# One launch of five blocks on one core: TensorE's order in the first four units and at the join of tower and attention, constants around the relay's end, VectorE's order before the scores

## What is computed

```python
h = L0_tok(tokens)                     # embedding, a decaying memory, 4 x (layer norm, 128->512 gelu, 512->128), head 128->64
h = h + L0_attn(layernorm(h))          # fast weights: q, k, v, rk, rv, beta, rbeta from one projection
h = h + L0_ffn(layernorm(h))           # 8 experts, 2 chosen for a sequence
h = h + L1_attn(layernorm(h))          # 8 heads; softmax of scores mixed with a positional softmax
h = h + L1_ffn(layernorm(h))           # 8 experts, 2 chosen for a token

# L0_attn, over the 16 rows in order (per head)
W = W + (bt * (vt - W @ kt)) * kt ;  z = W @ qt                 # fast memory
q_rec = softmax(hid) ; R = R + (bt * (vt - R @ kt)) * kt        # second memory
hid = z + R @ q_rec ;  out = hid @ out_W
```

## Time and profile before

| | us |
|---|---|
| median of 3 runs | 646.36 (645.65 to 647.98) |
| the profiled execution, device time | 644.59 |
| its span in the trace | 642.8 |
| PE busy in it | 566.9 (88%) |
| DVE, ACT, POOL busy | 426.9, 351.3, 350.2 |

### The profile page before, as it was taken

The page is one execution under the profiler, slowest core; times in us unless marked ns, Lnnn a source line. Parts: engine busy times, 40 slices in busy tenths (PEclk is TensorE's granted clock), DMA queues, the critical chain, the costliest instruction groups (busy, mean ns, idle before and its releaser), DMA issues.

```text
span 642.8 us, 12533 instructions
## 1 busy us (share of the span) xinstructions
PE 566.9 (88%) x4564; PEld 428.9 (67%) x4564; DVE 426.9 (66%) x1092; ACT 351.3 (55%) x914; POOL 350.2 (54%) x469
## 2 busy tenths in 40 slices
PE   7979999999899785777788878899998799999996
PEld 3547777777335674566777768786567577786686
DVE  4934564324766786899898888997226966666533
ACT  1064444442786763226787968730764557757430
POOL 1597663311810776879998999982666310001435
PEclk9979999999999999699999989999899899999999
DMA  7000000000000434200000000000000000000000
GB/s 277 8 1 1 2 0 1 1 1 1 1 1 2 75 77 65 77 0 2 2 1 2 0 2 1 2 1 1 1 1 2 2 1 2 1 2 2 6 12 17
DMA packets 10861, 10.45 MB, mean 16 GB/s; under 512 B 6000, under 2 KB 9840, under 8 KB 10544
## 3 DMA queue, kind: packets, MB, share of 16 engines
q1 hardware_dynamic: 8080, 7.54, 4.2%
q0 software_dynamic: 2144, 1.75, 1.5%
q10 hardware_dynamic: 576, 0.35, 0.2%
HBM read 5.77 MB, written 0.52 MB: 10 GB/s over the span
## 4 chain that ended last, share of the span: by engine, by line
PE 59%; DVE 16%; ACT 9%; POOL 6%; issue 4%; DMA 3%; SPq 1%; DVEq 0%; POOLq 0%; ACTq 0%
PE bank L1256 9%; PE bank L1244 8%; PE bank L1333 7%; PE bank L1548 5%; PE bank L1589 4%; DVE bank L2035 3%; DVE features L2029 2%; PE bank L1293 2%; PE bank L1496 2%; PE bank L1647 2%; PE bank L1303 2%; DVE features L2005 2%; PE bank L1324 1%; PE bank L1635 1%; SPq L450 1%
## 5 line engine op out<-in xcount | busy, mean ns | idle before, releaser
L1333 PE MATMUL bank<-ident,features 128*128 128x128 f32 x604 | 80.0, 284 | 10.3 <-DVE features L2005 5.6
L1333 PEld LDWEIGHTS bank<-ident,features 128*128 128x128 f32 x604 | 70.4, 147 | 17.5 <-DVE features L2005 11.5
L855 ACT ACTIVATE G<-bank,cols 128x512 f32<-128x512 f32 x64 | 43.6, 686 | 53.2 <-PE bank L1244 53.2
L1244 PE MATMUL bank<-xs,weights 128*128 128x512 f32 x128 | 60.5, 617 | 2.4 <-ACT xs L846 2.3
L590 POOL TENSOR_TENSOR features<-UV,coefs 128x1024 f32<-128x1024 f32 (+3 forms) x36 | 59.7, 1673 | 2.2 <-DVE UV L1992 2.2
L1256 PE MATMUL bank<-weights,G 128*128 128x128 f32 x512 | 59.8, 275 | 0.0
L1256 PEld LDWEIGHTS bank<-weights,G 128*128 128x128 f32 x512 | 58.4, 192 | 0.0
L2005 DVE TENSOR_TENSOR features<-UV,bank 128x1024 f32<-128x1024 f32 (+3 forms) x68 | 55.6, 861 | 1.6 <-PE bank L1333 0.8
L390 POOL TENSOR_SCALAR rstd<-mv 128x4 f32<-128x4 f32 x8 | 1.6, 194 | 96.2 <-DVE mv L402 96.2
L940 ACT ACTIVATE xs<-UV,coefs 128x32 f32<-128x32 f32 x232 | 50.3, 308 | 0.0
L940 ACT ACTIVATE sx<-UV,coefs 128x32 f32<-128x32 f32 x200 | 43.4, 307 | 0.0
(11 more groups left out here) (355 smaller groups left out, 1399.8 us busy)
## 6 DMA issues: line engine op xcount, KB each, us to landing
weights<-in_w SPq DMA_DIRECT2D x2, 1024.0 KB, 9.9
features<-in_tok SPq DMA_DIRECT2D x1, 768.0 KB, 5.9
weights<-in_ew SPq DMA_DIRECT2D x4, 128.0 KB, 3.3
weights<-in_ew SPq DMA_DIRECT2D x2, 256.0 KB, 3.0
coefs<-G POOLq DMA_DIRECT2D x16, 25.5 KB, 4.9
rows<-in_rows SPq DMA_DIRECT2D x1, 384.0 KB, 6.4
out_h<-H SPq DMA_DIRECT2D x3, 128.0 KB, 2.0
coefs<-G SPq DMA_DIRECT2D x14, 25.5 KB, 4.7
```

Of the source, the lines that this page charges most:

```text
L855: act.activation(G[:, 4 * (w % 2) + f, :], up_bank(f)[:], ACT.Gelu, bias=col("b1", 4 * i + f)).then_inc(s["tok_gelu"], 1)
L1244: mm(up_bank(f)[:], w1[:, i, P * f:P * f + P], xT[:, w % 2, :], start=True, stop=True).then_inc(s["tok_up"], 1)
L1333: last = mm(out[:, P * k:P * k + P], x[:, P * k:P * k + P], ident[:], is_transpose=True, start=first and k == 0, stop=last_ and k == n - 1 ...
```

## The change

Nothing is computed otherwise; orders on three engines change, and constants.

1. Units 0 to 3: ScalarE takes the gelus of unit 0 ahead of `unit_first(1)`, and in units 1 and 2 `unit_first` and `evict_T` stand between gelus. TensorE runs down(0) in two halves on either side of turn(1).
2. The join: `normalised(0)` goes ahead of down(15); the heads of chunks 2 and 3, with VectorE's parts and `a_norm(1)` to `a_norm(3)`, go between the features of chunks 0 and 1. ScalarE runs one exponential of a single column right after the last gelu.
3. Constants: at the relay 10 and 3 become 8, 4 (after a new wait for the softmax's factors) and 5; steps 0, 1, 2 get 4, 2, 2 behind the `rec` reads; row 12's third piece of `held` gets 6 ahead of it; in the scores 3 ahead of the loop and 2 after `turn_scores(0)` and `turn_scores(1)`.
4. Scores: VectorE takes `d_apply(1)` after `normalise(0)`, and `add_experts(3)` and what follows it one row later. TensorE's wait for that addition moves from ahead of the loop to `values_back(0)`.

```diff
@@ ACT
             evict_T(0)
-            for w in range(NU):
-                if w + 1 < NC:
-                    unit_first(w + 1)
+            gelus(0)
+            unit_first(1)
+            evict_T(1)
+            for w in range(1, NC - 1):
+                gelus(w, 0, 2)
+                unit_first(w + 1)
+                gelus(w, 2, 3)
+                evict_T(w + 1)
+                gelus(w, 3, 4)
+            for w in range(NC - 1, NU):
...
-            for c in range(1, NC):
-                head(c)
+            act.activation(decay[:, 3:4], ones[:, 0:1], ACT.Exp).then_inc(s["decay_exp"], 1)
+            head(1)
             normalised(0)
...
@@ PE
                 if w == 0:
                     embed(3)
+                    down(0, 0, 2)
...
-                if w:
+                if w == 0:
+                    down(0, 2, CH)
+                elif w > 1:
                     down(w - 1)
...
             head(1)
+            normalised(0)
             down(NU - 1)
-            for c in range(2, NC):
-                head_turn(c)
-                head(c)
...
+                    if t == 12 and r0 == 2 * CH:
+                        pe.wait_ge(s["o_add"], t - 1)
+                        warm(6)
                     pe.wait_ge(s["held_p"], i + 1)
...
-            for k in range(10):
-                mm(held_sum[:, HB:2 * HB], ident[:], RK[:, 0, :], start=True, stop=True)
+            constants(held_sum[:, HB:2 * HB], 8)
+            pe.wait_ge(s["p_done"], 1)
+            constants(held_sum[:, HB:2 * HB], 4)
             pe.wait_ge(s["p_done"], 2)
...
+            constants(held_sum[:, HB:2 * HB], 5)
...
                 read_out("rec", t, reads_of("rec", t))
+                if t < 3:
+                    pe.wait_ge(s["o_add"], t)
+                    warm((4, 2, 2)[t])
...
             fold_sums(3)
-            pe.wait_ge(s["y_read"], NC)
+            constants(bank[6][:, HB:2 * HB], 3)
...
                 turn_scores(t)
+                if t < 2:
+                    constants(bank[6][:, HB:2 * HB], 2)
@@ DVE
             for c in range(NC):
                 feature(c, 0)
                 feature(c, 1)
                 read_keys(CH * c)
+                if c == 0:
+                    a_norm(1)
+                    head(2)
+                    a_stats(2)
+                elif c == 1:
+                    a_norm(3)
...
                 f1_apply(c)
-                if c:
-                    d_apply(c - 1)
+                if c == 1:
+                    d_apply(0)
...
                 normalise(t)
                 if t == 0:
+                    d_apply(1)
+                if t == 1:
                     add_experts(chunk[NC - 1])
                     f1_stats(NC - 1)
```

More of the change, by code:

```diff
@@ L847, in evict_T, with gelus @@
                                scale=col("ln_g", i)).then_inc(s["tok_hT"], 1)
-            def gelus(w):
+            def gelus(w, f0=0, f1=4):
                 i, c = unit(w)
-                for f in range(4):
+                for f in range(f0, f1):
                     act.wait_ge(s["tok_up"], 4 * w + f + 1)
@@ L981, in _ @@
                     turned_keys(c - 1, 0)
+                else:
+                    head(3)
                 feature(c, 2)
@@ L1245, in up, with down @@
                        start=True, stop=True).then_inc(s["tok_up"], 1)
-            def down(w):
+            def down(w, j0=0, j1=CH):
                 i, c = unit(w)
@@ L1253, in down @@
                     pe.wait_ge(s["tok_add"], w - 1)
-                for j in range(CH):
+                for j in range(j0, j1):
                     for f in range(4):
@@ L1257, in down @@
                                   w2[:, i, f, :], start=(f == 0), stop=(f == 3))
-                last.then_inc(s["tok_down"], 1)
+                if j1 == CH:
+                    last.then_inc(s["tok_down"], 1)
             def head_turn(c):
@@ L1264, in head_turn @@
                     pe.wait_ge(s["head_xT"], c)
+                if c == 2:
+                    pe.wait_ge(s["a_turned"], 2)
                 for j in range(CH):
@@ L1279, in normalised @@
                 pe.wait_ge(s["a_norm"], c + 1)
-                pe.wait_ge(s["head_xT"], NC)
+                pe.wait_ge(s["head_xT"], NC if c else 2)
                 if c:
@@ L1423, in _ @@
             head(1)
+            normalised(0)
             down(NU - 1)
-            for c in range(2, NC):
-                head_turn(c)
-                head(c)
             pe.wait_ge(s["load_attn"], 64)
             pe.wait_ge(s["pad"], 1)
-            normalised(0)
             pe.wait_ge(s["tok_gelu"], 4 * NU)
-            pe.wait_ge(s["tok_add"], NU)
             for c in range(NC):
@@ L1435, in _ @@
                 feature(c, 1)
+                if c == 0:
+                    head_turn(2)
+                    pe.wait_ge(s["tok_add"], NU - 1)
                 values_keys(CH * c)
@@ L1438, in _ @@
                     turn_keys(c - 1, 0)
+                else:
+                    head(2)
+                    head_turn(3)
                 feature(c, 2)
+                if c == 0:
+                    pe.wait_ge(s["tok_add"], NU)
                 values_keys(CH * c + 1)
@@ L1469, in _ @@
                 last.then_inc(s["p_T"], 1)
-            for k in range(3):
-                mm(held_sum[:, HB:2 * HB], ident[:], RK[:, 0, :], start=True, stop=True)
+            constants(held_sum[:, HB:2 * HB], 5)
             def queries(t):
@@ L1666, in values_back @@
                 pe.wait_ge(s["av_saved"], p + 1)
+                if p == 0:
+                    pe.wait_ge(s["y_read"], NC)
                 if p % 2 == 0 and p:
@@ L2152, in _ @@
             a_stats(0)
+            a_norm(0)
             add(NU - 2)
-            a_norm(0)
             head(1)
@@ L2157, in _ @@
             add(NU - 1)
[L2158 to L2164, removed]
             for c in range(NC):
@@ L2168, in _ @@
                 read_keys(CH * c)
+                if c == 0:
+                    a_norm(1)
+                    head(2)
+                    a_stats(2)
+                elif c == 1:
+                    a_norm(3)
                 feature(c, 2)
                 read_keys(CH * c + 1)
+                if c == 0:
+                    head(3)
+                    a_stats(3)
                 feature(c, 3)
@@ L2173, in _ @@
                 read_keys(CH * c + 3)
+                if c == 0:
+                    a_norm(2)
             dve.wait_ge(s["rk_T"], 2 * NC)
@@ L2389, in _ @@
                 if t == 0:
+                    d_apply(1)
+                if t == 1:
                     add_experts(chunk[NC - 1])
                     f1_stats(NC - 1)
-                if t == 1:
+                if t == 2:
                     f1_apply(NC - 1)
                     d_stats(NC - 2)
-                if t == 2:
+                if t == 3:
                     d_apply(NC - 2)
-                if t == 3:
+                if t == 4:
                     d_stats(NC - 1)
-                if t == 4:
+                if t == 5:
                     d_apply(NC - 1)
```

## The result

In the first comparison the changed kernel took 639.58 us (median of 4 runs, 637.23 to 640.11) beside 647.17 for the kernel before (645.65 to 650.42): a ratio of 0.9857, interval 0.9818 to 0.9896. The profiled execution took 639.34 with a span of 637.6, so the two profiles differ by only 5.25. The forecast was a gain of 5.8.

A forecast was written before the change was run, and what follows sets the result against it. TensorE, busy 88%, was taken to set the pace mostly, with waits and half clock in early tower, join, recurrence and first scores; 1.6 - 3.5 - 0.3 - 0.85 - 2.75 = -5.8 from 646.36 gives 640.6, range 638.2 to 643.9.

The forecast's parts named there:

- The tower: Units 0 to 3: new order keeps 0.4 us of 4.4, half clock behind turn(4)'s wait costs 2.0; together +1.6.
- The rival that turn(4) does not wait: Tower: GpSimd's list runs earlier than thought, all 4.4 us stay, 634.6; chance 0.04.
- The join: Down(15) to chunk 1's features: they start 4.1 us sooner, less VectorE's norm delay; -3.5 taken.
- Relay and steps 0 to 2: Recurrence start: constants hold the clock, shortening the relay's constants and step 1; together -0.3 us.
- The first rival: Recurrence: constants do not hold the clock and cost double, +3.0 in place of -0.3, 643.9; chance 0.14.
- The rule of the Trainium skill: Recurrence: transpose mode does not engage full clock, so it falls between few constants; would give 643.9 rather than 640.6.
- Row 12: Recurrence: six constants fit the 3.15 us idle, transposes and turn behind run at full clock; -0.85 us.
- Scores: First scores: reordered norm, no TensorE wait or half clock, less two pairs of constants; -2.75 us.
- the base of 646.36: Whole kernel: median of the runs before, 1.77 above the profiled 644.59, from which the forecast subtracts 5.8.

The follow-up runs named there:

- e2: Changed kernel with GpSimd's fills of constants moved behind its root for unit 8: 635.39, ratio 0.9806 to the kernel before.
- e8: Changed kernel with VectorE's norms of chunks 2 and 3 one chunk later: 640.02, ratio 0.9876 to the kernel before.
- e4: Changed kernel with the join of before put back: ratio 0.9942 to the kernel before.
- e3: Changed kernel without the two pairs of constants behind the turned scores of rows 0 and 1: 639.25, ratio 0.9855 to the kernel before.
- c2: Changed kernel run again with nothing edited: 640.76, ratio 0.9889 to the kernel before.
- e6: Changed kernel without the six constants ahead of row 12's third piece: ratio 0.9891 to the kernel before.
- e1: Changed kernel with the old order of units 0 to 3 on ScalarE and TensorE: ratio 0.9872 to the kernel before.
- e7: Changed kernel with the first scores of before (VectorE's order, TensorE's wait, no constants there): ratio 0.9912 to the kernel before.
- c3: Kernel before, unchanged, profiled again: join and step 11 as in its first profile, relay 3.3 us longer; no run time given.
- c4: Kernel before, unchanged, profiled again: join 51.83 us, half clock twice as long in step 11; no run time given.
- e5: Changed kernel with the constants of before around the relay (ten and three) and none in steps 0 to 2: ratio 0.9863 to the kernel before.

## Why the prediction was right in its places and wrong in its sum

**The tower** went as written: turn(4) at 58.17 (forecast 58.25), behind an idle 3.82, with the half clock on turn(4) and down(2); up(4), at 64.75, ran at full clock again. The first profile has +2.2 to the end of the tower, the means of the table +1.6 (six towers in the old order 147.8, eight in the new 149.4): the term, +1.6. In the first profile the half clock lasted for 6.8 us there, in the seven others for 3.4. The rival that turn(4) does not wait is out, by e2, which had to remove the wait to see it go.

**The join** gave 2.7 where 3.5 was forecast from the first profile. The forecast was 4.1 less 0.6 for VectorE's norm, and 0.8 is missing. The start of chunk 1's features before, and the first two features of the changed kernel:

```profile
172.96 1.99 PE L1293 MATMUL bank<-coefs,sx 128*128 128x512 f32 x4
```
```profile
160.24 1.88 PE L1307 MATMUL bank<-coefs,sx 128*128 128x512 f32 x4
```

Counted from the last gelu, chunk 1's features start at 24.46 before and at 20.84 now: 3.6 earlier, not 4.1. TensorE, busy throughout, needed 11.3 from the end of down(15) at 160.24 to 171.57 for the list that was added up to 10.7; from one start to the next a head took 0.94, not 0.84. So 0.5 of the 0.8 is TensorE's own list, too small. The other 0.3 lies behind that point: there the new order loses 0.9, of which e8 gives back 0.68, the norm beside GpSimd, within the 0.3 to 1.3 that it was given and close to the 0.6 that was taken. But in three of five profiles of before, and in e4, the half clock falls into the old join, with its gaps between head and head; in none of the eleven profiles with the new heads between the features did it fall there. Against the mean of the old joins (51.65) the new one is worth 3.7. The term came out right by errors that cancel, which is luck.

**Relay and steps 0 to 2**: -0.3 was forecast, +0.1 measured (steps 0 to 4, means 38.10 and 38.16). The first rival's condition was met in part, in six of the eleven profiles with these constants: the clock was down on the two of step 1 in five of them (1.70 to 1.92 for 1.03, as in the row at 268.44) and on the four of step 0 in e3:

```profile
263.86 3.02 PE L1522 MATMUL bank<-RK,ident 128*128 128x256 f32 x8
```

Its price was too high: the stage took 37.87 to 38.18 in the five and 38.78 in e3, where c2 and e6, with the clock up all through it, took 37.79 and 37.80. That is 0.1 to 0.4 and 1.0, not 1.2 and 1.8. The 39.69 of e2 has another place: there the clock fell at 275.3, in step 3, on constants that the kernel before has as well. The rule of the Trainium skill that stood beside that rival (TensorE: Matmul & The Clock Gate, Part 4, PE-mode transpose) is not settled here: the rise at 275.0 goes against it; the falls in these steps, among transposes, could go with it.

**Row 12** was forecast at -0.85; the first two profiles give -0.99, and the means of steps 4 to 15 -1.5 (145.37 in six kernels without the constants, 143.89 in eleven with them). The price of that gap was taken from one half-clock stretch; in four of the six it lasted twice as long. Against that, the clock fell on step 12's own constants in two of the eleven (e1, e7).

**Scores**: -2.75 forecast, -2.80 measured, in the first pair and in the means.

**The step that failed** is that one profile of before stood for all of its runs, in the terms and in the sum: "The median of the runs is 1.77 above it; I make the forecast against the median". That takes the profiled execution as typical and its distance to the median as the same for both kernels. Of 64 runs of before 4 are shorter than its 644.59; the median is 3.5 above it. That of the changed kernel is 0.6 above its own. So the 5.25 that the profiles show, near the 5.8, became 8.1. That 5.25 is near 5.8 is itself in part luck: 0.93 of it lies in the experts, which the change does not touch, and the other stages make -4.3 (+2.2, -2.7, -0.1 for the relay with steps 0 to 4, -1.0, -2.8).

By the means of the stages the gain is +1.6 - 3.7 - 1.5 + 0.1 - 1.5 - 0.3 - 2.8 = -8.1 (tower, join, Gram matrices with the relay, steps 0 to 4, steps 4 to 15, experts, scores), as the pooled runs have it. So the forecast's term that was mis-sized most is row 12, -0.85 for a measured -1.5, because the one profile had the shorter of two stretches of half clock there; and the Gram matrices with the relay (-1.5) and the experts (-0.3) had been put at nothing. As a time, 640.6 is 1.0 above the first median and 0.6 above the pooled one; there the base of 646.36, 1.7 below the pooled median of before, and the gain, 2.3 too small, cancel, which is luck. As a gain over that base, 0.9857 makes 637.1, below the range.

**Open** is whether that -1.5 belongs to the change. The stage goes from 57.2 to 61.7 in both groups (five profiles of before, mean 60.2; twelve others, 58.7). The three longest (c3 and c4 of before, e3 of the changed kernel: 61.5 to 61.7) are the three in which the clock was down for 12.5 to 13.7 us of it; in the other fourteen it was down for 3.4 to 10.2. Whether the change makes such stretches rarer there, twelve against five profiles can't tell. e5 alone touches the stage, by the constants at the relay; its 59.69 lies inside both groups.

## What to carry to other kernels

A profile is one draw: before a forecast is made against it, look where its time lies among the runs, and price a gap on TensorE by how often the clock falls there, not by whether it fell in the one trace. Closing gaps with real work (the join) paid in every profile. Of the constants that were tested apart, those over the gap of 3.15 us (row 12) paid; those of steps 0 to 2 and the pairs at the scores did not, and where the clock was down two of them took 1.92 for 1.03. And when an order is improved up to a wait, the next thing to move is what stands ahead of the awaited instruction in its own queue: here fills that nobody needed yet.

## What the runs showed that was not expected

The half clock came and went at the same instructions: in the experts of the changed kernel the clock stayed up, and in e5, with the same instructions there, it fell at 443, though PE had just been busy for 6.49 of 7.0 us with the last reads' transposes, the turns of the rows and one-column products. The windows and a row of e5:

```profile
436.00:443.00 7.00, 6.49 (x63) 4.97 (x61) 5.39 (x23) 0.98 (x2) 1.26 (x2) 1.00 0.00 0
443.10:449.90 6.80, 6.53 (x23) 4.21 (x24) 2.34 (x11) 0.39 (x2) 1.16 (x2) 0.50 0.01 2
262.20:275.80 13.60, 10.59 (x43) 8.77 (x44) 12.05 (x30) 2.70 (x9) 12.26 (x26) 0.50 0.10 26
```
```profile
446.26 4.20 PE L1588 MATMUL bank<-RK,ident 128*128 128x256 f32 x10
```

No gap of some us stands ahead of this one, unlike the falls of the earlier trace rows. It cost the stage 3.0 (49.07 for 46.06), with ten matmuls for constants on the path at 4.20 (2.42 in the changed kernel). And VectorE's four scalings took 2.44 and 2.51 at the join beside GpSimd's additions of two tensors, as the 2.37 in the earlier trace rows, for 1.1 alone.
